# Two turned graph aggregations in three chunks of 512, 512 and 226 nodes for four, with the edge work one node tile later

## The chip, the cores and the metric

The kernel runs on one core of one Trainium2 chip. The metric is the device time of one execution in microseconds (us), taken over several runs. The engines are named as the profile names them: PE (matrix products; PEld are its weight loads), DVE (vector work), ACT (activations and copies), POOL (here almost wholly the issue of DMAs) and SP (nothing but DMA issues). A DMA is a transfer by the 16 DMA engines that all queues share.

## The reference

There are 1250 nodes with 1024 features and 20000 edges (src, dst), sorted by dst. All products are 1024 by 1024.

```
deg_inv = 1 / max(in-degree by dst, 1)
mean(h) = segment_sum(h[src], dst) * deg_inv
h   = relu(x @ W_self0 + mean(x) @ W_neigh0 + b0)
y   = layernorm(x + h @ W_self1 + mean(h) @ W_neigh1 + b1)
z   = y @ W.T + b                       # third layer: edges turned (src gathers dst), self loops added
out = layernorm(y + segment_sum(norm * z[dst], src)),   norm = dsqrt[src] * dsqrt[dst]
```

## The kernel before

**Adjacency as dense panels.** Sums over edges are done as matrix products with a 1250 by 1250 matrix of edge counts, padded to 10 node tiles of 128 and stored in DRAM as five panels of two tiles (256 columns, 1.28 MB each). There are two of them, adj_in (for the first two layers) and adj_out (for the third). POOL clears each with four large DMAs (L634) and then fills it by 160 indirect DMAs (the function put, L641), one for each column of 125 edges, all on one queue, first the 160 of adj_in and then those of adj_out. The 160 fall in 10 groups of 16; since the edges are sorted by dst, group g holds the edges whose dst is about 125g to 125g+125. A group may be put when DVE has finished repeats(g), which finds edges that occur more than once; its last instruction raises batch_ready (L980). Puts of adj_in raise one of the semaphores scattered_in, split by NEEDS: the numbers of groups after which the first, second, ... chunk of node columns is complete.

**Stages on PE.** (1) N0: x @ W_neigh0, ten node tiles one after the other (function linear, L1409). Each tile of x is first turned by PE (turn_tile), copied as a high part by ACT (turn_hi, L682) and a low part by DVE (turn_lo, L900). Results are split by evict_hi and evict_lo. In between, DVE does the edge work in the order its loop gives: edge_keys (waits for the edge list's DMA), edge_cells, edge_form, repeats. A one-column product (the small sum, L1402) on PE adds up the bad flags that edge_keys makes, for edge_form. (2) S0: x @ W_self0, turned, in three chunks CHUNKS0 of 4, 4 and 2 tiles (L1437); its blocks go to DRAM (s0t_scr). (3) The first turned aggregation, mean0 (L1468): for each chunk of CHUNKS, degrees by a product with ones (L1457), then for each of the eight feature blocks d twenty matmuls against the chunk's panels; the results stand in six PSUM banks in rotation, so block m waits for h_free m-5. DVE multiplies a block by 1/degree (L1169, which raises h_free), then adds the stored S0 block that SP has fetched (L1172, which waits for s0_in and raises h_sum), and so on in order; ACT applies the relu. (4) Two big products by a seven-product scheme (L1525). (5) MEAN1 (L1542). (6) The second turned aggregation, gather (L1559), against adj_out, chunk by chunk, each followed by a sum of scale factors (L1581) that waits for ten steps of DVE (L1281). (7) GCN: the last product, ten node tiles (L1409 again), with layer normalization and stores.

**SP's queue is in order.** The lines below are the part of SP's program that feeds stage 3. load_chunk_1(c) loads the panels of chunk c, after waits on the scatters of all groups that the chunk needs; what follows in the program, the fetches of S0 blocks (L512) among them, waits behind it.

```python
            sp.wait_ge(m1_full[0], 16)
            load_chunk_1(1)
...
            for m, (c, d) in enumerate(H_BLOCKS):
...
                sp.dma_start(fetch_slot(m)[:, 0:CHUNKS[c][1] * T], s0t_scr[d, :, lines(CHUNKS[c])]).then_inc(s0_in[m % 8], 16)
                if m in (15, 23):
                    load_chunk_1(2 + m // 17)
```

In the kernel before, chunks 0, 1, 2 and 3 of mean0 hold 256, 512, 256 and 226 nodes and need 3, 7, 9 and 10 groups.

Of the kernel before, what the change touches and what calls it, by code (L numbers as in the profile page):

```python
# [23 lines left out]
def build(nc, x, src, dst, w_self0, w_neigh0, b0, w_self1, w_neigh1, b1, w_gcn, b_gcn, out):  # L24
# [29 lines left out]
    MEAN1_PAIRS = (1, 2, 0, 1, 2, 0, 1, 2, 0, 2)  # L54
# [9 lines left out]
    PRODUCT_BANKS = ((0, 1, 2, 3, 4), (0, 1, 2, 3, 4), (5, 6, 7, 0, 1), (2, 3, 4, 5, 6), (7, 0, 1, 2, 3), (7, 0, 1, 2, 3), (4, 5, 6, 7, 0))  # L64
    assert NT == 2 * HALF and KD == 2 * KH and HALF == 5 and XOP + WOP <= OPS and HD == BANK

    with ExitStack() as ctx:
# [127 lines left out]
        def product_bank(g, i, p):  # L195
            return (PRODUCT_BANKS[i][p] + g) % 8

# [32 lines left out]
        def acc_pair(q, t):  # L230
            if q == N0:
                return t % 2
            if q == GCN:
                return (1, 3, 0)[t % 3]
            return MEAN1_PAIRS[t]

# [26 lines left out]
        scattered_in = sems("scattered_in", 4)  # L263
# [6 lines left out]
        m1_full = sems("m1_full", 4)  # L270
        p1_full = sems("p1_full", 3)
        m2_full = sems("m2_full", 4)
# [79 lines left out]
        for l in (N0, S0, GCN):  # L352
            for k in range(KD):
                raw_slot[l, k] = 4 + k % 2 if l == GCN else 2 + k if l == N0 and k >= 4 else k % 4
                loads[raw_slot[l, k]] += 1
                raw_count[l, k] = loads[raw_slot[l, k]]
# [4 lines left out]
        H_BLOCKS = [(c, d) for c in range(4) for d in range(KD)]  # L361
# [13 lines left out]
        def fetch_free(m):  # L375

            return m - 3 if m < 2 * KD else 2 * KD - 3 + m % 8 // 2 if m < 3 * KD else m - 7
# [31 lines left out]
        def _(sp):  # L409
# [9 lines left out]
            def load_panels(table, c, where, full):  # L419
                t0, n = CHUNKS[c]  # L420
# [5 lines left out]
            def load_tile(t):  # L426
                sp.dma_start(g_tile[:, t % 2, :, :].bitcast(F32), xt_scr[t, :, :, :]).then_inc(xt_full[t % 2], 16)
# [21 lines left out]
            def load_chunk_1(c):  # L449
                if c == 0:  # L450
                    sp.wait_ge(*last_use(6))
                elif c == 1:
                    sp.wait_ge(s0_full, 3 * KD)
                else:
                    sp.wait_ge(h_full, KD * (c - 1))
                    sp.wait_ge(dsum_done, sum(n for _, n in CHUNKS[:c - 1]) // 2)
# [18 lines left out]
            for i, (c, k) in enumerate(S0_STEPS):  # L475
# [24 lines left out]
                if i == 21:  # L500
                    load_chunk_1(0)
            sp.wait_ge(m1_full[0], 16)
# [4 lines left out]
            for m, (c, d) in enumerate(H_BLOCKS):  # L507
                for i in [S0_BLOCKS.index((b, d)) for b in {0: (0,), 1: (0, 1), 2: (1,), 3: (2,)}[c]]:
                    sp.wait_ge(s0_stored[i % 4], 16 * (i // 4 + 1))
                if m >= 4:  # L510
                    sp.wait_ge(h_sum, fetch_free(m))
                sp.dma_start(fetch_slot(m)[:, 0:CHUNKS[c][1] * T], s0t_scr[d, :, lines(CHUNKS[c])]).then_inc(s0_in[m % 8], 16)  # L512
                if m in (15, 23):
                    load_chunk_1(2 + m // 17)
# [10 lines left out]
            sp.wait_ge(h_sum, KD * 4)  # L525
# [36 lines left out]
            load_panels(adj_out, 0, m2_panels[0], m2_full)  # L562
# [17 lines left out]
            for t in range(NT):  # L580
                if t == 0:
                    sp.wait_ge(g_full, KD * 3)
                    sp.wait_ge(s_step, NT * 3)
                    for j in range(4):
                        sp.wait_ge(g_stored[j], 16 * 2)
                if t >= 2:
                    sp.wait_ge(acc_full, acc_index(GCN, t - 2) + 1)
                if t in [t0 for t0, n in CHUNKS[1:]]:
                    c = [t0 for t0, n in CHUNKS].index(t)
# [3 lines left out]
                if t == 1:  # L593
                    sp.wait_ge(w_lo_done, KD * GCN + 6)
                    load_w(GCN, 7)
                    for j in range(4):
                        sp.wait_ge(g_stored[j], 16 * KD)
                    sp.wait_ge(g_full, KD)
                    sp.wait_ge(s_step, NT)
                    for s in range(2):  # L600
                        sp.wait_ge(stored[s], 16 * NT // 2)
                        sp.dma_start(xin[:, s, :], y_scr[node_rows(s), :]).then_inc(res_full[s], 16)
                if t >= 2:
                    sp.wait_ge(acc_free, acc_index(GCN, t - 2) + 1)
                    sp.dma_start(xin[0:rows(t), t % 2, :], y_scr[node_rows(t), :]).then_inc(res_full[t % 2], 16)
# [71 lines left out]
        def _(act):  # L677
# [964 lines left out]
```

## Time and profile before

| what | value |
|---|---|
| median of 3 runs | 859.11 us (858.87 to 862.55) |
| the profiled execution, own time | 865.72 us |
| span of its trace, first to last instruction | 863.9 us |
| mean granted PE clock | 0.988 |
| PE busy | 838.9 us |
| POOL busy | 460.4 us |

The profile is of one execution, whose own time is 6.6 us above the median and 1.8 us above its span. A matmul's end is modelled, so differences of starts are the better measure of a rate. A clock of 1.0 is 2.4 GHz, 0.5 is 1.2 GHz; a number between is a mean over the stretch. "Idle before" names what ended an engine's wait, inferred from semaphores; "issue" means nothing that the profile shows.

### The profile page before, as it was taken

To read this page: it belongs to the slowest core of one execution; us is meant where nothing else is said; L and a number is where in the kernel's file an instruction comes from. 1 tells how busy PE (TensorE), PEld (TensorE's weight loads), DVE (VectorE), ACT (ScalarE), POOL (GpSimd) and SP (SyncE) were. 2 spreads that over 40 slices of the span, in tenths; PEclk is the share of its full clock that TensorE was granted. 3 is DMA by queue.
4 is the path that set the end of the run, shared out by engine and by line. 5 is a ranking of instruction groups with operands and counts; after the bars stand their busy time and mean duration, and the time that the engine had idled before them with its cause. 6 is when DMAs were issued, how large, how long until landed. Compare 5 with 4: busy or idle time off the path is not lost.

```text
span 863.9 us, 10999 instructions
## 1 busy us (share of the span) xinstructions
PE 838.9 (97%) x4295; PEld 714.8 (83%) x4295; DVE 461.6 (53%) x714; ACT 177.8 (21%) x218; POOL 460.4 (53%) x343
## 2 busy tenths in 40 slices
PE   8799999999999999999999999999999999999996
PEld 6588888888899889888888888778889789988885
DVE  5486567100015655698654478766655535455554
ACT  5011113020211111652303201312222213200000
POOL 4038886877878868886788788878720000000000
PEclk9899999999999999999999999999999999999999
DMA  9968938363578354388688477448778748655551
GB/s 297 384 244 313 315 112 263 95 197 80 150 214 265 80 134 109 93 322 288 240 278 316 155 284 255 102 127 219 213 248 276 224 147 274 226 195 195 195 189 44
DMA packets 99482, 180.56 MB, mean 209 GB/s; under 512 B 15474, under 2 KB 75898, under 8 KB 94048
## 3 DMA queue, kind: packets, MB, share of 16 engines
q1 hardware_dynamic: 60144, 124.17, 43.3%
q10 hardware_dynamic: 26896, 40.65, 13.3%
q0 software_dynamic: 12384, 14.95, 7.6%
q8 instruction: 38, 0.62, 0.3%
q14 instruction: 20, 0.16, 0.1%
HBM read 107.08 MB, written 72.43 MB: 208 GB/s over the span
## 4 chain that ended last, share of the span: by engine, by line
PE 86%; DMA 5%; DVE 4%; ACT 2%; issue 2%; ACTq 1%; POOL 0%; DVEq 0%; SPq 0%; POOLq 0%
PE ps L1409 22%; PE ps L1525 19%; PE ps L1437 12%; PE ps L1559 10%; PE ps L1468 10%; PE ps L1542 9%; DMA u<-edges_scr 3%; PE ps L1393 1%; DMA spare<-in_x 1%; ACT outb L743 1%; PE ps L1358 1%; PE ps L1348 1%; DMA edges_scr<-u 1%; PE ps L1457 1%; ACTq L733 0%
## 5 line engine op out<-in xcount | busy, mean ns | idle before, releaser
L641 POOL DMA_INDIRECT adj_out<-loops,idx_out x160 | 244.3, 1527 | 70.8 <-issue 64.6
L641 POOL DMA_INDIRECT adj_in<-mult,idx_in x160 | 200.4, 1252 | 89.3 <-issue 89.3
L1525 PE MATMUL ps<-u 128*128 128x512 f32 x840 | 190.7, 389 | 1.4 <-DVE u L1064 1.4
L1525 PEld LDWEIGHTS ps<-u 128*128 128x128 f32 x840 | 157.6, 188 | 34.2 <-issue 1.6
L1409 PE MATMUL ps<-wx 128*128 128x512 f32 x480 | 115.7, 399 | 1.7 <-ACT wx L700 1.2
L1437 PE MATMUL ps<-wx 128*128 128x512 f32 (+1 forms) x576 | 111.0, 355 | 1.6 <-ACT outb L743 1.6
L1437 PEld LDWEIGHTS ps<-wx 128*128 128x128 f32 x576 | 95.5, 193 | 17.1 <-ACT outb L743 2.1
L1409 PEld LDWEIGHTS ps<-wx 128*128 128x128 f32 x480 | 90.8, 192 | 22.3 <-ACT wx L700 2.3
L1409 PE MATMUL ps<-u 128*128 128x512 f32 x432 | 98.2, 389 | 0.0
L1542 PE MATMUL ps<-u,panel_tiles 128*128 128x512 f32 (+1 forms) x400 | 95.5, 398 | 1.9 <-DVE s L1131 1.9
L1468 PE MATMUL ps<-wx,u 128*128 128x256 f32 (+5 forms) x640 | 96.1, 312 | 0.0
L1409 PEld LDWEIGHTS ps<-u 128*128 128x128 f32 x432 | 81.0, 188 | 16.8
L1468 PEld LDWEIGHTS ps<-wx,u 128*128 128x128 f32 (+1 forms) x640 | 88.1, 194 | 6.6
L1542 PEld LDWEIGHTS ps<-u,panel_tiles 128*128 128x128 f32 (+1 forms) x400 | 75.6, 191 | 18.5 <-issue 2.3
L1559 PE MATMUL ps<-u,wx 128*128 128x512 f32 (+2 forms) x480 | 74.5, 317 | 0.0
L1559 PEld LDWEIGHTS ps<-u,wx 128*128 128x128 f32 x480 | 67.2, 191 | 6.6
L1161 DVE TENSOR_SCALAR dinv_row<-ps 128x256 f32<-128x256 f32 (+2 forms) x4 | 1.9, 479 | 99.3 <-PE ps L1457 99.3
L826 ACT ACTIVATE std<-mv,eps 128x1 f32<-128x1 f32 x20 | 5.9, 295 | 165.5 <-DVE mv L1007 165.5
L743 ACT ACTIVATE outb<-ps,b0c 128x512 f32<-128x512 f32 (+1 forms) x24 | 14.8, 618 | 102.2 <-PE ps L1437 90.3
L1325 DVE SCALAR_TENSOR_TENSOR outb<-ps,dscale,xin 128x1024 f32<-128x1024 f32 x9 | 11.6, 1284 | 40.6 <-PE ps L1409 40.6
L798 ACT ACTIVATE ht<-ht 128x256 f32<-128x256 f32 (+2 forms) x32 | 14.9, 465 | 80.3 <-DVE ht L1172 80.3
L1169 DVE TENSOR_TENSOR ht<-ps,dinv_row 128x256 f32<-128x256 f32 (+2 forms) x32 | 15.3, 479 | 25.3 <-PE ps L1468 25.1
(168 smaller groups left out, 737.7 us busy)
## 6 DMA issues: line engine op xcount, KB each, us to landing
left_scr<-u SPq DMA_DIRECT2D x7, 2560.0 KB, 9.7
u<-left_scr SPq DMA_DIRECT2D x7, 2560.0 KB, 9.6
xt_scr<-wx ACTq DMA_DIRECT2D x10, 1024.0 KB, 9.9
u<-xt_scr SPq DMA_DIRECT2D x10, 1024.0 KB, 4.9
wx<-xt_scr SPq DMA_DIRECT2D x16, 512.0 KB, 3.6
adj_in<-u POOLq DMA_DIRECT2D x4, 1600.0 KB, 22.9
adj_out<-u POOLq DMA_DIRECT2D x4, 1600.0 KB, 14.1
wx<-adj_in SPq DMA_DIRECT2D x5, 1280.0 KB, 6.8
```

The costliest lines, as they stand in the source:

```text
L641: pool.indirect_dma_start(table, bass.IndirectOffsetOnAxis(ap=index[0:EP, j:j + 1], axis=0), counts[0:EP, j:j + 1], None, bounds_check=CEL ...
L743: nc.scalar.activation(staged[i % 4][:, 0:width], ps[:, d, 0:width], ACT.Identity, bias=b0c[:, d:d + 1]).then_inc(s0_free, 1)
L798: nc.scalar.activation(cell, cell, ACT.Relu).then_inc(h_done, 1)
L1169: nc.vector.tensor_tensor(cell, ps[:, h_bank(m), 0:width], row, ALU.mult).then_inc(h_free, 1)
L1325: nc.vector.scalar_tensor_tensor(z, pair_bank(acc_pair(GCN, t))[:, :], dscale[:, t:t + 1], rest, ALU.mult, ALU.add).then_inc(acc_free, 1)
L1348: ins = nc.tensor.transpose(ps[:, 4 + k // 4, k % 4 * T:(k % 4 + 1) * T], xin[:, t % 2, k * P:(k + 1) * P], ident[:, :])
L1409: ins = nc.tensor.matmul(acc[:, cols], left_tile[:, t % 2, k, left * T:(left + 1) * T], w_row(q, k, right)[:, cols], start=(i == 0), stop= ...
L1437: ins = nc.tensor.matmul(block_of[d], w[:, k, left, d * P:(d + 1) * P], where[right], start=(first and left + right == 0), stop=(final and ...
L1468: ins = nc.tensor.matmul(ps[:, h_bank(m), 0:width].rearrange("p (n j) -> p n j", n=n // 2), typed(u0_part(k, h, d), exact), typed(panels[0 ...
L1525: ins = nc.tensor.matmul(ps[:, product_bank(g, i, p), :], left_op[n % 2][:, p, k, left, :], right_op[n % 2][:, k, right, :], start=(not on ...
L1542: ins = nc.tensor.matmul(pair_bank(acc_pair("MEAN1", t))[:, cols], typed(p1_tile[t][0:rows(k), k, :], exact), typed(u[0:rows(k), n, k, h, ...
L1559: ins = nc.tensor.matmul(ps[:, g_bank(KD * c + d), 0:width].rearrange("p (n j) -> p n j", n=n // 2), typed(yd[:, h, d * P:(d + 1) * P], ex ...
```

## The change

Both turned aggregations go over three chunks instead of four. mean0 uses CHUNKS0: 512, 512 and 226 nodes, which need 5, 9 and 10 groups of edges. gather takes the small chunk (226 nodes) first, then 512 and 512. Panels of two chunks of mean0 and of the gather move to other addresses; the weight rows of the last product that these addresses overlap are split later (rows 3 and 4 after the gather's second chunk, rows 5 to 7 after its end). The last product takes its node tiles in the order of LAST_TILES. In stage 1, edge_keys moves from the end of node tile 0 to tile 1 (behind turn_lo(2)), edge_cells and edge_form from tile 1 to tile 2, repeats(0) from tile 1 to tile 3, and the small sum on PE from tile 1 to tile 2. PSUM banks are renamed to suit (MEAN1_PAIRS, BANK_ORDER), and the counts in waits are adapted. The diff, cut to its core:

```diff
-    CHUNKS = ((0, 2), (2, 4), (6, 2), (8, 2))
     CHUNKS0 = ((0, 4), (4, 4), (8, 2))
-    NEEDS = (3, 7, 9, GROUPS)
+    CHUNKS = ((8, 2), (0, 4), (4, 4))
+    NEEDS = (5, 9, GROUPS)
+    LAST_TILES = (0, 1, 8, 9, 2, 3, 4, 5, 6, 7)
...
-    MEAN1_PAIRS = (1, 2, 0, 1, 2, 0, 1, 2, 0, 2)
+    MEAN1_PAIRS = (0, 1, 2, 0, 1, 2, 0, 1, 0, 2)
+    BANK_ORDER = (4, 5, 0, 1, 2, 3, 6, 7)
...
-        m1_panels = [panels_at(wx, OPS + PSIZE * i, n) for i, n in ((0, 1), (1, 2), (0, 1), (2, 1))]
+        m1_panels = [panels_at(wx, OPS + PSIZE * i, n) for i, n in ((0, 2), (2, 2), (0, 1))]
-        m2_panels = [panels_at(panel_tiles, PER, 1), panels_at(u_flat, XT_AT - 2 * PSIZE, 2), panels_at(u_flat, XT_AT, 1),
-                     panels_at(u_flat, XT_AT - PSIZE, 1)]
+        m2_panels = [panels_at(panel_tiles, PER, 1), panels_at(u_flat, XT_AT - 4 * PSIZE, 2), panels_at(u_flat, XT_AT - 2 * PSIZE, 2)]
...
-            return (PRODUCT_BANKS[i][p] + g) % 8
+            return BANK_ORDER[(PRODUCT_BANKS[i][p] + g) % 8]
...
-        H_BLOCKS = [(c, d) for c in range(4) for d in range(KD)]
+        H_BLOCKS = [(c, d) for c in range(3) for d in range(KD)]
...
             def load_chunk_1(c):
                 if c == 0:
-                    sp.wait_ge(*last_use(6))
+                    sp.wait_ge(*last_use(7))
...
                 for b in range(c + 1):
                     sp.wait_ge(scattered_in[b], 16 * RUN * (NEEDS[b] - (NEEDS[b - 1] if b else 0)))
-                load_panels(adj_in, c, m1_panels[c], m1_full)
+                load_panels(adj_in, CHUNKS0[c], c, m1_panels[c], m1_full)
...
-                if i == 21:
+                if i == 23:
                     load_chunk_1(0)
-            sp.wait_ge(m1_full[0], 16)
+            sp.wait_ge(m1_full[0], 32)
             load_chunk_1(1)
...
-                if m in (15, 23):
-                    load_chunk_1(2 + m // 17)
+                if m == 15:
+                    load_chunk_1(2)
...
-            for c in range(1, 4):
-                if c == 3:
-                    sp.wait_ge(g_full, KD * 2)
-                    sp.wait_ge(s_step, NT * 2)
-                load_panels(adj_out, c, m2_panels[c], m2_full)
-                for k in {1: (2, 3), 2: (4, 5), 3: (6,)}[c]:
-                    sp.wait_ge(w_lo_done, KD * GCN + k - 1)
-                    load_w(GCN, k)
+            for c in range(1, 3):
+                load_panels(adj_out, CHUNKS[c], c, m2_panels[c], m2_full)
+            for k in (2, 3, 4):
+                sp.wait_ge(w_lo_done, KD * GCN + k - 1)
+                load_w(GCN, k)
...
+                elif l == GCN and k < 3:
+                    act.wait_ge(acc_full, acc_index("MEAN1", NT - 1) + 1)
                 elif l == GCN and k < 5:
-                    act.wait_ge(acc_full, acc_index("MEAN1", NT - 1) + 1)
-                elif l == GCN and k == 5:
                     act.wait_ge(g_full, 2 * KD)
                     act.wait_ge(s_step, 2 * NT)
                 elif l == GCN:
-                    act.wait_ge(g_full, 32)
-                    act.wait_ge(s_step, 4 * NT)
+                    act.wait_ge(g_full, 3 * KD)
+                    act.wait_ge(s_step, 3 * NT)
...
                     turn_lo(t + 1)
                     if t == 1:
+                        edge_keys()
+                    elif t == 2:
                         edge_cells()
                         edge_form()
-                        repeats(0)
-                    elif t >= 2:
-                        repeats(t - 1)
+                    elif t >= 3:
+                        repeats(t - 3)
                     evict_lo(N0, t)
-                    if t == 0:
-                        edge_keys()
...
-            for g in range(NT - 2, GROUPS):
+            for g in range(NT - 4, GROUPS):
                 repeats(g)
...
-                    if q == N0 and t == 1 and i == 20:
+                    if q == N0 and t == 2 and i == 16:
                         pe.wait_ge(bad_ready, 1)
```

## Rows read from the trace of the kernel before

**Rows 1.** The page: busy time of the engines, first line

```profile
PE 838.9 (97%) x4295; PEld 714.8 (83%) x4295; DVE 461.6 (53%) x714; ACT 177.8 (21%) x218; POOL 460.4 (53%) x343
```

**Rows 2.** Timeline of PE, 0 to 70 us: start, us, instructions [idle before]

```profile
39.53 0.19 PE L1402 MATMUL ps<-ones_nt,bad 125*1 125x1 f32 x2 [6.11 <-DVE bad L920]
39.65 6.48 PE L1409 MATMUL ps<-wx 128*128 128x512 f32 x16
...
46.75 11.17 PE L1409 MATMUL ps<-wx 128*128 128x512 f32 x48
...
58.56 11.15 PE L1409 MATMUL ps<-wx 128*128 128x512 f32 x48
```

**Rows 3.** Windows: PE, PEld, DVE, ACT, POOL busy us; PE clock; DMA share, GB/s

```profile
39.50:46.10 6.60, 6.57 (x20) 5.17 (x21) 5.14 (x15) 1.02 (x1) 0.00 (x0) 0.57 1.01 431
```

**Rows 4.** Timeline of DVE, 8 to 100 us

```profile
36.30 1.32 DVE L910 SCALAR_TENSOR_TENSOR key<-u 125x1120 f32<-125x1120 int32 x1 [10.90 <-DMA u<-edges_scr]
...
47.27 0.96 DVE L968 TENSOR_TENSOR same_eq<-key 125x768 f32<-125x768 f32 x1
...
52.02 0.17 DVE L980 TENSOR_TENSOR idx_in<-idx_in,repeat 125x16 int32<-125x16 int32 x1
...
71.67 1.23 DVE L900 TENSOR_TENSOR wx<-ps,wx 128x1024 fp32r<-128x1024 f32 x1 [1.40 <-ACT wx L682]
```

**Rows 5.** The four clears of adj_in on POOL (line L634), issued 21.0 to 22.7 us

```profile
L634 POOL DMA_DIRECT2D adj_in<-u x4: 532/548/598, 21.0 to 22.7; - x4
...
DMA to landing us min/median/max: 18.1/22.9/32.7
```

**Rows 6.** Timeline of POOL, 0 to 200 us: the first scatter, and a pause

```profile
56.39 1.28 POOL L641 DMA_INDIRECT adj_in<-mult,idx_in  x1 [33.19 <-issue]
...
140.55 1.70 POOL L641 DMA_INDIRECT adj_in<-mult,idx_in  x1 [5.86 <-issue]
```

**Rows 7.** Windows of line L641 alone: scatters counted; then that line, 287 us on

```profile
56.30:289.30 233.00, 179.33 (x144) 0.99 0.63 194
...
L641 POOL DMA_INDIRECT adj_in<-mult,idx_in x2: 1192/1194/1196, 286.5 to 288.0; - x2
```

**Rows 8.** Line L641 over the whole span: issue to landing

```profile
DMA to landing us min/median/max: 2.5/3.5/21.0
```

**Rows 9.** Timeline of SP's DMA queue, 205 to 360 us

```profile
250.23 1.09 SPq L423 DMA_DIRECT2D wx<-adj_in  x2
251.42 5.32 SPq L512 DMA_DIRECT2D xin<-s0t_scr  x1
```

**Rows 10.** Timeline of DVE, 250 to 345 us

```profile
257.64 0.36 DVE L1169 TENSOR_TENSOR ht<-ps,dinv_row 128x256 f32<-128x256 f32 x1
264.55 0.42 DVE L1172 TENSOR_TENSOR ht<-ht,xin 128x256 f32<-128x256 f32 x1 [6.55 <-DMA xin<-s0t_scr]
```

**Rows 11.** Timeline of PE, 246 to 360 us: each chunk's degrees (L1457), then the products

```profile
251.96 1.43 PE L1457 MATMUL ps<-wx,ones_r 128*128 128x256 f32 x10 [1.80 <-ACT outb L743]
...
274.62 2.46 PE L1457 MATMUL ps<-wx,ones_r 128*128 128x512 f32 x10
...
314.80 1.35 PE L1457 MATMUL ps<-wx,ones_r 128*128 128x256 f32 x10
...
335.91 1.28 PE L1457 MATMUL ps<-wx,ones_r 128*128 128x226 f32 x10
...
357.20 2.97 PE L1525 MATMUL ps<-u 128*128 128x512 f32 x12 [1.43 <-DVE u L1064]
```

**Rows 12.** Timeline of PE, 645 to 752 us: the gather

```profile
671.56 0.61 PE L1581 MATMUL ps<-ones_nt,sacc 128*128 128x1 f32 x4 [0.72 <-DVE sacc L1281]
672.02 36.99 PE L1559 MATMUL ps<-u,wx 128*128 128x512 f32 x160
...
709.66 19.43 PE L1559 MATMUL ps<-u,wx 128*128 128x256 f32 x160
...
729.29 18.11 PE L1559 MATMUL ps<-u,wx 128*128 128x226 f32 x160
```

More of the change, by code:

```diff
@@ L353, in build @@
             for k in range(KD):
-                raw_slot[l, k] = 4 + k % 2 if l == GCN else 2 + k if l == N0 and k >= 4 else k % 4
+                raw_slot[l, k] = 1 if l == GCN and k == KD - 1 else 4 + k % 2 if l == GCN else 2 + k if l == N0 and k >= 4 else k % 4
                 loads[raw_slot[l, k]] += 1
@@ L417, in load_w, with load_panels @@
                 sp.dma_start(raw_slots[slot], weights[l][k * P:(k + 1) * P, :]).then_inc(raw_full[slot], 16)
-            def load_panels(table, c, where, full):
-                t0, n = CHUNKS[c]
+            def load_panels(table, chunk, c, where, full):
+                t0, n = chunk
                 for i in range(n // 2):
@@ L593, in _ @@
                 if t == 1:
[L594 to L602, printed above, removed]
+                    for k in (5, 6):
+                        sp.wait_ge(w_lo_done, KD * GCN + k - 1)
+                        load_w(GCN, k)
                 if t >= 2:
                     sp.wait_ge(acc_free, acc_index(GCN, t - 2) + 1)
-                    sp.dma_start(xin[0:rows(t), t % 2, :], y_scr[node_rows(t), :]).then_inc(res_full[t % 2], 16)
+                    sp.dma_start(xin[0:rows(tile), t % 2, :], y_scr[node_rows(tile), :]).then_inc(res_full[t % 2], 16)
             sp.wait_ge(stored[0], 16 * NT)
@@ L771, in right_high @@
                 if n < 2:
-                    act.wait_ge(h_full, KD * 3 + KH if n == 0 else KD * 4)
+                    act.wait_ge(h_full, KD * 2 + KH if n == 0 else KD * 3)
                 else:
@@ L865, in _ @@
                     store_g(m - 1)
-                if m in (4, 8, 12, 16, 20, 24):
-                    split_hi(GCN, m // 4 - 1)
-            store_g(31)
-            split_hi(GCN, 6)
-            split_hi(GCN, 7)
+                if m in (7, 9, 11, 18, 20):
+                    split_hi(GCN, (7, 9, 11, 18, 20).index(m))
+            store_g(23)
+            for k in range(5, KD):
+                split_hi(GCN, k)
             for t in range(NT):
@@ L875, in _ @@
                 s = t % 2
+                tile = LAST_TILES[t]
                 if t < NT - 1:
                     act.wait_ge(norm_done, NT + t + 1)
-                    act.dma_start(out[node_rows(t), :], outb[0:rows(t), s, :]).then_inc(stored[s], 16)
+                    act.dma_start(out[node_rows(tile), :], outb[0:rows(tile), s, :]).then_inc(stored[s], 16)
                 else:
@@ L882, in _ @@
                         act.wait_ge(norm_done, NT + t + 1 + n)
-                        act.dma_start(out[node_rows(t), cols], outb[0:rows(t), s, cols]).then_inc(stored[s], 16)
+                        act.dma_start(out[node_rows(tile), cols], outb[0:rows(tile), s, cols]).then_inc(stored[s], 16)
         @block.vector
@@ L915, in edge_keys @@
                 then_next(nc.vector.tensor_tensor(mult[0:EP, :], mult[0:EP, :], loops[0:EP, :], ALU.add))
-                for (t0, n), g in list(zip(CHUNKS, NEEDS))[:-1]:
+                for (t0, n), g in list(zip(CHUNKS0, NEEDS))[:-1]:
                     then_next(nc.vector.scalar_tensor_tensor(mult[0:1, 0:1], e_dst[0:1, g, WINDOW:WINDOW + 1], float((t0 + n) * T),
@@ L1185, in _ @@
                     right_sums(0, 0)
-                elif m == 27:
+                elif m == 19:
                     left_low(0)
@@ L1302, in _ @@
                     scale_done(c)
-                if m in (4, 8, 12, 16, 20, 24):
-                    split_lo(GCN, m // 4 - 1)
-            split_lo(GCN, 6)
-            split_lo(GCN, 7)
+                if m in (7, 9, 11, 18, 20):
+                    split_lo(GCN, (7, 9, 11, 18, 20).index(m))
+            for k in range(5, KD):
+                split_lo(GCN, k)
             for t in range(NT):
@@ L1366, in pair_free @@
                 elif q == "MEAN1":
-                    pe.wait_ge(acc_free, acc_index(q, 7 if t == NT - 1 else t - 3) + 1)
+                    pe.wait_ge(acc_free, acc_index(q, max(i for i in range(t) if MEAN1_PAIRS[i] == MEAN1_PAIRS[t])) + 1)
                 elif q == GCN and t < 3:
-                    pe.wait_ge(g_free, 28 + 2 * t)
+                    pe.wait_ge(g_free, 20 + 2 * t)
                 elif q == N0:
@@ L1447, in mean0 @@
             def mean0(exact):
-                for c, (t0, n) in enumerate(CHUNKS):
+                for c, (t0, n) in enumerate(CHUNKS0):
                     width = node_cols((t0, n))
@@ L1480, in product_bank_free @@
                 if i == 0 and g == 0:
-                    pe.wait_ge(h_free, 27 + p)
+                    pe.wait_ge(h_free, 19 + p)
                 elif i == 0 and p < 3:
@@ L1488, in product_bank_free @@
                 elif i == 2 and p < 3 and g == 0:
-                    pe.wait_ge(h_free, 32)
-                    pe.wait_ge(dcol_read, 4)
+                    pe.wait_ge(h_free, 24)
+                    pe.wait_ge(dcol_read, 3)
                 elif i == 2 and p < 3:
```

69 lines of the change are left out of this document (36 added, 33 removed).

## The prediction, made before the changed kernel ran

> **What bounds the kernel now.** I read the page first: PE is busy 97% of the span [rows 1], so a gain must be a PE wait that goes or PE work that shrinks, and a loss must be a new PE wait. Next the list of waits and PE's timeline: the one wait of any size is the small sum, which waits 6.11 us for the bad flags [rows 2]. DVE makes them, and DVE sits 10.90 us until the edge list lands at 36.30 [rows 4]. Then POOL, because the change asks for more groups of scatters earlier: POOL is no bottleneck by its busy time, but its 160 scatters of adj_in are a serial chain from 56.39 to past 300 us [rows 6, 7], and mean0 (252 to 357 us) lives off it. Last SP, DVE and PE around mean0 [rows 9 to 11], and PE in the gather [rows 12].
>
> **The change part by part.**
>
> *The small sum one tile later.* Its wait goes: the flags need the edge list (36.30) and 3.2 us of DVE, so 39.5; without the wait PE finishes tile 1 at 33.4 + 8 matmuls, about 35.2 (a tile's 48 matmuls and eight turns take 58.56 - 46.75 = 11.81 us [rows 2]; 0.23 us a matmul), and reaches step 16 of tile 2 near 43.5, when the flags lie ready. The wait also cost its aftermath: the 16 matmuls behind it took 6.48 us where 16 take 3.7 at 0.23 each, at a mean granted clock of 0.57, a mix of the two levels after 6 us of idle PE [rows 2, 3]. So PE gains 6.1 + 2.8 = 8.9 us by the end of N0, and mean0 can start at about 243 instead of 251.96 [rows 11]. Bounds: 6.1 if the clock falls anyway, 8.9 if not; I take 8.9, as nothing else stops PE there.
>
> *The edge work later.* repeats(0) now stands two tiles later in DVE's program, but DVE is no longer held by the edge list ahead of turn_lo(2). Tile 3 now starts at 35.2 + 11.8 = 47.0, and PE turns tile 4 at 48.8. DVE's turn_lo came 2.1 us after such a turn (the turn behind the last of the 48 matmuls from 58.56, at 69.6, and turn_lo at 71.67 [rows 2, 4]), so 50.9 to 52.1; repeats takes 52.19 - 47.27 = 4.9 us [rows 4], so group 0 is ready at 57.1, against 52.2. POOL's first scatter had waited for the last clear: 22.7 + 32.7 = 55.4, then 1.0 us to the put at 56.39 [rows 5, 6]. Now it starts at 58.1, some 2 us later. Bounds: 0 (the clear still ends last) and +6 (DMA is full until about 47 us [rows 3], and the store that turn_hi(4) waits for can be late). Nothing behind changes: one group of 16 takes 24 us of POOL and 5 of DVE.
>
> *Five and nine groups.* In the kernel before, 144 scatters (nine groups) had been issued by 288.0 [rows 7]; with 2 us and the median 3.5 to landing [rows 8] they land at T = 293.5. Chunk 1 of mean0 now needs these nine groups; before it needed seven. mean0 now starts at 243, and its first chunk takes what a 512 chunk takes, 314.80 - 274.62 = 40.2 us [rows 11], so PE wants chunk 1 at 283. That is 10 us before its edges are in DRAM. This wait sits in SP, and SP is in order: behind load_chunk_1(1) stand the fetches of S0 blocks, so chunk 0's additions on DVE wait too. In the kernel before, the same sequence took 264.55 - 250.23 = 14.3 us from the issue of the two panels to the first addition [rows 9, 10], the fetch landing behind the panels. So DVE adds block 0 at T + 14.3 = 307.8, multiplies block 1 at 309.2 (0.7 us each), and only that frees PE's block 7 (h_free 2). PE comes to block 7 at 243 + 40.2 less one block of 4.6, so 278.6, and idles some 30 us. It comes back at the low clock: block 7 costs 16 matmuls at 6.48 and 4 at 0.9, 7.4 us, so 316.6. The panels have landed by then, and DVE, which has two panel sums (about 3 us each) and a second fetch to work off, frees block 8's bank before PE has done the degrees. Chunk 1: 40.2, to 356.8. Chunk 2 up to the first product: 357.20 - 335.91 = 21.3 [rows 11], its last link being the same DVE work, to 378.1. Before: 357.20. **Loss up to the products: 20.9 us.** The 8.9 us gained in N0, and the merged chunks of mean0 (22.7 + 21.1 for two of 256, 40.2 for one of 512: 3.6 us), are used up in waiting for T.
>
> *The gather.* Two chunks of 256 cost 160 matmuls at 120 ns (709.66 plus 19.3), one of 512 costs 160 at 230 (672.02 plus 36.9), one of 226 at 112 [rows 12]. Merging saves 2 x 19.3 - 36.9 = 1.7. But the chunk that goes first is followed by a wait for DVE's ten steps (PE waits 0.72 for them [rows 12]), which start when the first six blocks are done, 120 matmuls in: a first chunk of 226 instead of 256 columns brings that forward by 120 x 8 ns = 1.0, and the 0.3 of the other 40 matmuls is lost in the wait. I take 1.7 - 0.4 = **1.3 us gained**; bounds 0.4 (the first chunk gains nothing) and 1.7. The Trainium skill, page "TensorE: Matmul & The Clock Gate", section "Back-to-back issue gap", gives N/2.4 + 2.5 ns: 109 ns for 256 columns and 216 for 512, so that merging two would give 2.6 ns per pair, 0.4 us for 160; by it the sum below would be about 1 us longer. The rows (120, 230) differ from it and decide.
>
> *At nothing.* The weight rows 5 to 7 are split after the gather's end, each by a copy on ACT and a subtraction on DVE of turn_lo's size (1.23 [rows 4]): about 3 us for the last block's own copies, then 1.2 a row, so the third is done some 6.6 us after the end. PE takes 4 matmuls for each of rows 0 and 1 and 6 for each later one (0.23 us each), so it asks for rows 5, 6 and 7 at about 6.7, 8.1 and 9.4 us: cover 2.5 us, beyond that PE waits one for one. The scatters of adj_out run some 2 us later, the PE work that hides them some 20 us later, so their cover grows. The four panels of the gather's two larger chunks are issued together at MEAN1's end and hide behind the first chunk (19 us) and the second (37 us); two panels and what follows took 14.3 us above. Order of tiles, bank names: same instructions.
>
> **Sum.** 20.9 - 1.3 = +19.6 us. On the profiled execution: span 863.9 to 883.5, own time 865.7 to 885.3. The runs lie 6.6 us below that execution; with the same difference to the median, 859.1 + 19.6 = **878.7 us**.
>
> **The rivals.**
>
> *Scatters in time (faster).* One mechanism: the ninth group lands so early that SP never holds PE. Then everything counts: 8.9 + 3.6 + 1.3 = 13.8, so 845. For it: POOL pauses (5.86 us at one put [rows 6]) and slow puts may not come again. Against: PE asks for h_free 2 at 278.6, so T + 15.7 must be below that, T = 263, 30 us earlier than worked out. Even 144 puts at the undisturbed 1.5 us (24 us a group) from 58.1, with the 2.5 us of the clears of adj_out in between, end at 277. It decides only from T = 274 down (there loss and gains cancel). 0.08.
>
> *Only the panels are late.* If the additions do not hold PE (fetches in before the wait, or h_free ahead of it), PE does all of chunk 0 and waits just for the panels, T + 12 = 305.5: 305.5 + 40.2 + 21.3 = 367.0, +9.8 - 1.3 = +8.5, so 867.6. Against it: DVE's order, and the 14.3 us [rows 9, 10]. 0.12.
>
> *Later still.* Group 0 at +6, panels and fetches slower together, or the weight rows uncovered: +4 to +8, so 883 to 887. 0.08.
>
> *The wait is there but small (same).* T near 276 by faster puts: 859 within 4. 0.04.
>
> **How the numbers follow.** The forecast has 0.68: 878.7, with T from -8 (the pauses gone) to +4, so 870 to 883. The range for 8 in 10 takes in most of the two neighbours: 864 to 885. About 0.5% (4.3 us) is what a measurement tells here. Faster 0.08, same 0.04, slower 0.68 + 0.12 + 0.08 = 0.88.
>
> **What would show it.** Right: PE's wait on bad is gone and the clock in 33 to 46 us is whole; a PE wait of 25 to 32 us at a L1468 block in mean0, ended by DVE's L1169, with a low clock behind it; SP's issue of two adj_in panels near 293; the first put near 58; products from about 378; the gather some 1 us shorter. Wrong: puts at another pace, nine groups landed well before 290, or SP issuing the S0 fetches ahead of the panels; then the time moves one for one with T.

## The result, and the profile after

The changed kernel takes **878.23 us** (median of 4 runs, 877.63 to 879.50) against 860.77 beside it (858.87 to 862.55): ratio **1.0197**, 95% interval 1.0168 to 1.0227, so some 17 us slower. The forecast was 878.7. The profiled execution took 877.63, with a span of 875.9.

The page's chain of work that ended last, its two lines (by engine, by line):

```profile
PE 58%; POOL 18%; issue 10%; DMA 9%; DVE 3%; ACT 1%; SPq 1%; POOLq 0%; ACTq 0%; DVEq 0%
PE ps L1521 19%; POOL adj_in L636 17%; PE ps L1405 11%; PE ps L1555 10%; PE ps L1538 9%; PE ps L1464 6%; DMA adj_in<-u 4%; DMA first_rows<-in_L_gnn_W_neigh 2%; DMA spare<-in_x 1%; PE ps L1389 1%; DMA xin<-s0t_scr 1%; PE ps L1354 1%; DMA xt_scr<-outb 1%; POOLq L636 0%; DVE spare L1132 0%
```

The scatters of adj_in (L636, L641 before) are now 17% of the chain: from the first put to the 144th it holds only them and the gaps between them (part of its "issue"). Ahead of them stands the clear of adj_in ("DMA adj_in<-u", 4%). PE's waits (engine, line and what it waited for: us in total, times, longest):

```profile
PE ps L1464 <- DVE ht L1164: 22.9, 1, 22.9
PE ps L1577 <- DVE sacc L1276: 3.4, 1, 3.4
PE ps L1453 <- DMA wx<-adj_in: 2.8, 1, 2.8
```

The wait for bad [rows 2] is not among them. PE's timeline, N0 and then mean0 (compare [rows 2, 11]):

```profile
42.69 0.19 PE L1398 MATMUL ps<-ones_nt,bad 125*1 125x1 f32 x2
...
241.61 2.55 PE L1453 MATMUL ps<-wx,ones_r 128*128 128x512 f32 x10 [2.78 <-DMA wx<-adj_in]
...
258.83 18.63 PE L1464 MATMUL ps<-wx,u 128*128 128x512 f32 x80
300.35 6.90 PE L1464 MATMUL ps<-wx,u 128*128 128x512 f32 x20 [22.90 <-DVE ht L1164]
307.09 2.46 PE L1453 MATMUL ps<-wx,ones_r 128*128 128x512 f32 x10
...
347.33 1.28 PE L1453 MATMUL ps<-wx,ones_r 128*128 128x226 f32 x10
```

The small sum runs at 42.69 without a wait, and the granted clock around it (33 to 46 us) is 1.00. mean0 starts at 241.61, does 140 of its first chunk's 160 matmuls, and stops 22.9 us for h_free at block 7. The 20 matmuls behind the stop take 6.90 us at a clock of 0.67. Windows, 33 to 46 us and behind the stop (columns as in [rows 3]):

```profile
33.00:46.00 13.00, 13.00 (x63) 10.52 (x63) 9.19 (x25) 2.06 (x2) 0.00 (x0) 1.00 1.00 418
...
300.30:307.00 6.70, 6.65 (x20) 5.30 (x21) 2.60 (x2) 0.69 (x2) 5.22 (x5) 0.67 1.07 350
```

What releases that stop, read backwards through three timelines: DVE, SP, POOL (compare [rows 6, 7, 9, 10]):

```profile
299.00 0.69 DVE L1167 TENSOR_TENSOR ht<-ht,xin 128x512 f32<-128x512 f32 x1 [49.27 <-DMA xin<-s0t_scr]
299.61 0.68 DVE L1164 TENSOR_TENSOR ht<-ps,dinv_row 128x512 f32<-128x512 f32 x1
...
287.23 1.08 SPq L425 DMA_DIRECT2D wx<-adj_in  x2
288.41 2.82 SPq L514 DMA_DIRECT2D xin<-s0t_scr  x1
...
58.83 1.27 POOL L636 DMA_INDIRECT adj_in<-mult,idx_in  x1 [36.28 <-issue]
...
248.68 1.19 POOL L636 DMA_INDIRECT adj_in<-mult,idx_in  x1 [2.48 <-issue]
...
58.70:286.00 227.30, 175.29 (x144) 0.99 0.54 164
```

DVE frees the bank by the multiplication at 299.61, behind its first addition, which sat 49.27 us until the first S0 block was there. That fetch left SP at 288.41, behind two adj_in panels that SP could only ask for at 287.23. The 144 scatters of nine groups, from 58.83, are all put by 286 (the last row counts the puts in a window).

The gather, PE's timeline and one line of ACT's (compare [rows 12]):

```profile
661.06 18.20 PE L1555 MATMUL ps<-panel_tiles,wx 128*128 128x226 f32 x160
682.65 0.61 PE L1577 MATMUL ps<-ones_nt,sacc 128*128 128x1 f32 x4 [3.39 <-DVE sacc L1276]
683.12 38.58 PE L1555 MATMUL ps<-u,wx 128*128 128x512 f32 x160
...
722.35 36.98 PE L1555 MATMUL ps<-u,wx 128*128 128x512 f32 x160
...
680.78 0.38 ACT L857 ACTIVATE outb<-ps 128x256 fp32r<-128x256 f32 x1 [4.29 <-DMA xt_scr<-outb]
```

It takes 98.9 us (661.06 to 759.98) against 96.2. The wait behind its first chunk grew from 0.72 to 3.39, and the first 512 chunk takes 1.6 us more than the second, at a granted clock of 0.83 in its first 10 us.

### The profile page after: what moved, and what is told of

The parts are those of the page before. It is cut to its first block, busy times and chain, and to the rows that moved or that the text cites. A ratio compares the mean times of both kernels' runs of the same rounds, so it can differ in the third digit from the quotient of the medians.

```text
span 875.9 us, 10210 instructions
## 1 busy us (share of the span) xinstructions
PE 830.5 (95%) x3965; PEld 692.8 (79%) x3965; DVE 455.5 (52%) x675; ACT 174.8 (20%) x202; POOL 450.5 (51%) x343
## 4 chain that ended last, share of the span: by engine, by line
PE 58%; POOL 18%; issue 10%; DMA 9%; DVE 3%; ACT 1%; SPq 1%; POOLq 0%; ACTq 0%; DVEq 0%
PE ps L1521 19%; POOL adj_in L636 17%; PE ps L1405 11%; PE ps L1555 10%; PE ps L1538 9%; PE ps L1464 6%; DMA adj_in<-u 4%; DMA first_rows<-in_L_gnn_W_neigh 2%; DMA spare<-in_x 1%; PE ps L1389 1%; DMA xin<-s0t_scr 1%; PE ps L1354 1%; DMA xt_scr<-outb 1%; POOLq L636 0%; DVE spare L1132 0%
## 5 line engine op out<-in xcount | busy, mean ns | idle before, releaser
L636 POOL DMA_INDIRECT adj_out<-loops,idx_out x160 | 240.4, 1502 | 75.2 <-issue 70.4
L636 POOL DMA_INDIRECT adj_in<-mult,idx_in x160 | 194.4, 1215 | 90.6 <-issue 90.6
L1464 PE MATMUL ps<-wx,u 128*128 128x512 f32 (+1 forms) x480 | 94.9, 358 | 22.9 <-DVE ht L1164 22.9
L1405 PE MATMUL ps<-wx 128*128 128x512 f32 x480 | 113.2, 393 | 2.6 <-ACT wx L695 2.0
L1464 PEld LDWEIGHTS ps<-wx,u 128*128 128x128 f32 x480 | 79.4, 192 | 37.0 <-DVE ht L1164 23.3
L1433 PEld LDWEIGHTS ps<-wx 128*128 128x128 f32 x576 | 93.9, 189 | 16.8 <-ACT outb L738 1.8
L1405 PEld LDWEIGHTS ps<-wx 128*128 128x128 f32 x480 | 88.9, 188 | 22.5 <-ACT wx L695 3.5
L1555 PE MATMUL ps<-u,wx 128*128 128x512 f32 (+1 forms) x320 | 75.6, 398 | 0.0
L1555 PEld LDWEIGHTS ps<-u,wx 128*128 128x128 f32 (+1 forms) x320 | 61.2, 192 | 13.6
L1167 DVE TENSOR_TENSOR ht<-ht,xin 128x512 f32<-128x512 f32 (+1 forms) x24 | 14.2, 594 | 54.1 <-DMA xin<-s0t_scr 53.4
L793 ACT ACTIVATE ht<-ht 128x512 f32<-128x512 f32 (+1 forms) x24 | 13.3, 553 | 107.6 <-DVE ht L1167 107.6
```

The lines of the kernel that those rows point to most:

```text
L636: pool.indirect_dma_start(table, bass.IndirectOffsetOnAxis(ap=index[0:EP, j:j + 1], axis=0), counts[0:EP, j:j + 1], None, bounds_check=CEL ...
L793: nc.scalar.activation(cell, cell, ACT.Relu).then_inc(h_done, 1)
L1167: nc.vector.tensor_tensor(cell, cell, fetch_slot(m)[:, 0:width], ALU.add).then_inc(h_sum, 1)
L1405: ins = nc.tensor.matmul(acc[:, cols], left_tile[:, t % 2, k, left * T:(left + 1) * T], w_row(q, k, right)[:, cols], start=(i == 0), stop= ...
L1433: ins = nc.tensor.matmul(block_of[d], w[:, k, left, d * P:(d + 1) * P], where[right], start=(first and left + right == 0), stop=(final and ...
L1464: ins = nc.tensor.matmul(ps[:, h_bank(m), 0:width].rearrange("p (n j) -> p n j", n=n // 2), typed(u0_part(k, h, d), exact), typed(panels[0 ...
```

## The experiments

**Theory A**: T, the time from which SP may ask for chunk 1's panels (nine groups landed), sets the start of the products one for one, through SP's order and DVE's first addition. PE time won before it is spent in waiting. **Rivals**: the parts of the change simply add up; or the stop has another cause (the panels, the fetches, the banks of a 512 chunk) and would be there with the scatters in time.

Times are medians; ratios are to the kernel before on the same chip, with 95% intervals.

| run | us | ratio | what it is |
|---|---|---|---|
| e1_edges_only | 855.04 | 0.9935 (0.991 to 0.9961) | edge work and small sum later, alone |
| e10_edges_again | 854.25 | 0.9924 (0.9901 to 0.9946) | the same |
| e2_mean0_only | 879.33 | 1.0216 (1.0189 to 1.0242) | three-chunk mean0 alone |
| e3_gather_only | 865.16 | 1.0036 (1.0009 to 1.0062) | three-chunk gather alone |
| e9_old_gather | 877.72 | 1.0203 (1.0174 to 1.0233) | changed kernel, gather as before |
| e5_edges_early | 882.72 | 1.0226 (1.0184 to 1.0268) | changed kernel, edge work as before |
| e4_fetch_first | 877.52 | 1.0190 (1.0164 to 1.0217) | changed kernel, S0 fetches ahead of the panels |
| e6_puts_later | 893.50 | 1.0367 (1.0322 to 1.0412) | changed kernel, groups 5 to 9 put later |
| e7_two_groups_out | 857.59 | 0.9946 (0.9923 to 0.9969) | changed kernel, two groups of edges left out |
| e8_edges_gather_split | 854.18 | 0.9903 (0.9871 to 0.9936) | e1 with a gather in three chunks, panels in two steps |
| e11_edges_split_again | 857.60 | 0.9946 (0.9922 to 0.9971) | the same |
| e12_before_again | 863.40 | - | kernel before, second profile |

**The parts alone.** e1 takes this part of the change, e2 and e3 the others:

```diff
                     if t == 1:
+                        edge_keys()
+                    elif t == 2:
                         edge_cells()
                         edge_form()
-                        repeats(0)
-                    elif t >= 2:
-                        repeats(t - 1)
+                    elif t >= 3:
+                        repeats(t - 3)
```

> The kernel before with the edge work and the small sum one node tile later, and nothing else of the change. Theory A (the loss of the whole change is the wait for nine groups of scatters, and what PE gains ahead of it is used up there): alone the move is worth its full gain, since chunk 1 of mean0 still needs seven groups: PE's wait for the bad flags and the low clock behind it go, some 9 us, so about 852. Rival B (the later edge work makes the scatters late, and that is the loss): no gain or a loss, 860 or more, with new PE waits in mean0.

> The kernel before with the three chunks in the first aggregation alone. Theory A: the whole loss is here. PE comes to its block 7 some 9 us later than in the changed kernel, but goes on at the same time, since nine groups land when they land: a PE wait of about 14 to 18 us at a block of mean0, products near 366 to 369, 874 to 878 in all. Rival B (late edge work): the scatters start at 56 as before, so hardly any loss, 857 to 862.

> The kernel before with the three chunks in the gather alone (small one first, order of the last tiles). The prediction's term was 1.3 us gained, 859.5. The trace of the changed kernel shows instead a 3.4 us wait behind the first chunk and a gather 2.7 us longer than before: 863.5. If the wait there came from the late start of the whole kernel's second half, it is not seen here and 859.5 stands.

mean0 alone carries the whole loss (+18.6 us by its ratio), the edge work alone gains 5.6 to 6.5, the gather alone loses 3.1 (its wait behind the first chunk is 3.47 in e3, as in the changed kernel). Added up the three make about +16, next to the whole's +17, so these times alone do not tell theory A from the rival that the parts add up. The products do: in e2 they start at 372.50, and 10.6 us (what e1 gains, below) earlier would be 361.9, but the changed kernel has them at 368.62. e1's PE timeline, mean0's start, its third chunk and the products; last, from e2's PE timeline, its products:

```profile
241.35 1.43 PE L1459 MATMUL ps<-wx,ones_r 128*128 128x256 f32 x10 [1.93 <-ACT outb L746]
...
304.22 1.35 PE L1459 MATMUL ps<-wx,ones_r 128*128 128x256 f32 x10
...
346.61 33.57 PE L1527 MATMUL ps<-u 128*128 128x512 f32 x147 [1.43 <-DVE u L1066]
...
372.50 22.72 PE L1529 MATMUL ps<-u 128*128 128x512 f32 x99 [1.47 <-DVE u L1068]
```

Products at 346.61 against 357.20 [rows 11]: without the three chunks the 10.6 us won in N0 reach the products whole. In the times only 5.6 to 6.5 of them show (855.04, where 852 was expected): the execution behind [rows 11] lay 4.1 us above the 861.62 beside e1, and e1's profiled one 1.7 below its own median. The chunk that needs nine groups starts at 304.22 and waits for nothing.

**The edge work back, inside the change** (the diff above, undone):

> The changed kernel with the edge work and the small sum back at their old places; both three-chunk aggregations stay. Theory A (the landing of the nine groups, T, sets the products' start, so PE time won in N0 is spent in waiting): PE stops again for the flags in N0, but the time stays within 3 us of the changed kernel's 878, 875 to 881; the wait in mean0 gets shorter by about what N0 loses. Theory B (the parts add up): the 5.7 us that the edge work gave alone are lost again, about 884.

The median lies nearest to B (884); by the ratios e5 is 2.5 us above the changed kernel, and its interval takes in both A's 881 and B's 884. The trace says A, with T itself moved. e5's stop in mean0, the issue of the panels, the products and a pause of POOL:

```profile
303.55 6.69 PE L1468 MATMUL ps<-wx,u 128*128 128x512 f32 x20 [13.77 <-DVE ht L1168]
...
290.72 1.08 SPq L428 DMA_DIRECT2D wx<-adj_in  x2
...
371.97 16.34 PE L1525 MATMUL ps<-u 128*128 128x512 f32 x71 [1.44 <-DVE u L1063]
...
252.10 1.20 POOL L639 DMA_INDIRECT adj_in<-mult,idx_in  x1 [6.02 <-issue]
```

mean0 starts 10.8 us later (252.38 against 241.61), and the stop shrinks from 22.90 to 13.77: 9.1 are absorbed. But T is 3.5 us later, although the first put is earlier (55.39 against 58.83), since POOL pauses 6.02 us where it paused 2.48, and loses 3.4 us more in the rest of the 144 puts (1.3 of it at an earlier pause, 5.24 for 3.98). In 244 to 254 us the DMA engines are 85% busy in e5 (mean0's first panels are loaded then, 10 us later than in the changed kernel) and 20% busy in the changed kernel. So of the edge work's gain inside the change, what is left comes by way of T.

**The old gather, inside the change:**

> The changed kernel with the gather in its old four chunks: the later edge work and the three-chunk mean0 alone. If the gather's three chunks cost 3 us, as they did alone and as the two traces show (98.9 against 96.2 us): 875, between 873 and 877. If the gather's loss is only a shift of what comes before it: 878 as the changed kernel.

877.72, ratio 1.0203: no difference from the changed kernel that the times can tell. In e9's trace the gather takes 96.2 us, and its wait is 0.73, so the 2.7 us stand in the traces. Alone (e3) they came out as 3.1 in the time. From the products to the end, the six traces with this gather (the changed kernel, e3 to e7) take 506.9 to 510.7 us and the six with the old one (the kernel before twice, e1, e2, e9, e10) 505.1 to 506.8: 3.3 us apart in the mean. In the time of the full change this cost is not settled.

**The dose: the puts 12 us later.**

```diff
             for g in range(GROUPS):
                 pool.wait_ge(batch_ready, g + 1)
+                if g == 4:
+                    pool.wait_ge(cleared_out, 16 * 4)
+                    for i in range(2):
...
+                        pool.dma_start(diagonal, ones_nt[:, 0:NT // 2], allow_slow_non_contiguous=True).then_inc(diagonal_set, 16)
+                    pool.wait_ge(diagonal_set, 32)
+                    for j in range(4):
+                        put(adj_out, idx_out, loops, j, scattered_out)
```

> The changed kernel, with the two diagonal writes and the first four scatters of adj_out moved from behind the 160 scatters of adj_in to before its fifth group of sixteen; the same work, but the groups 5 to 9 of adj_in are put some 6 us (the diagonal and its landing) plus 6 us (four scatters) later. Theory A: the nine groups land about 12 us later, and the time moves with it one for one: 878 + 12 = 890, between 887 and 893; the wait in mean0 grows from 22.9 to about 35 us. Rival (the wait comes from the panels and the fetches that share the DMA engines, or from the bank order, whenever the groups land): 878 to 881.

```profile
314.14 7.07 PE L1470 MATMUL ps<-wx,u 128*128 128x512 f32 x20 [33.23 <-DVE ht L1170]
...
301.33 1.08 SPq L428 DMA_DIRECT2D wx<-adj_in  x2
...
382.96 5.24 PE L1527 MATMUL ps<-u 128*128 128x512 f32 x22 [1.44 <-DVE u L1065]
...
262.73 1.19 POOL L639 DMA_INDIRECT adj_in<-mult,idx_in  x1 [2.41 <-issue]
```

In e6's timelines of PE, SP and POOL the panels are asked for 14.1 us later (the moved work costs 13.2 us at its place, where 12 were expected), the stop is 33.23, the products start 14.3 us later, and the median moves by 15.3 (893.5, half a microsecond above the range given). One for one, as far as the times tell: theory A.

**The wait taken away: two groups left out.**

```diff
-            for g in range(GROUPS):
+            for g in (0, 1, 2, 3, 4, 5, 6, 9):
...
-                    sp.wait_ge(scattered_in[b], 16 * RUN * (NEEDS[b] - (NEEDS[b - 1] if b else 0)))
+                    sp.wait_ge(scattered_in[b], 16 * RUN * (5, 2, 1)[b])
```

> The changed kernel without the scatters of groups 7 and 8 of adj_in (32 of 160): that part of the edges is left out of the first two layers' sums, and the second chunk's panels wait for the seven remaining groups of its nine. They land some 48 us earlier, near 245. Theory A: no PE wait in mean0, all that the change saves on PE shows: products start near 241.5 + 40.5 + 40.5 + 21 = 343.5 against 368.6, so 878 - 25 = 853, between 850 and 856. Rival (a first chunk of 512 columns also stops for the panels, the fetches or the banks): a wait of 8 us or more stays, 860 or above.

```profile
244.03 3.96 PE L1456 MATMUL ps<-wx,ones_r 128*128 128x512 f32 x10 [2.99 <-DMA wx<-adj_in]
...
285.88 2.48 PE L1456 MATMUL ps<-wx,ones_r 128*128 128x512 f32 x10
...
326.07 1.28 PE L1456 MATMUL ps<-wx,ones_r 128*128 128x226 f32 x10
...
347.37 32.92 PE L1524 MATMUL ps<-u 128*128 128x512 f32 x144 [1.43 <-DVE u L1062]
```

No stop inside mean0; the products start at 347.37 and the time falls by 20.6. The rival that a 512 chunk stops anyway is out. It missed 853 by 4.6: products 3.9 us later than expected, and a second half 1.9 us longer than the changed kernel's. And it shows something else. The four runs with the edge work later and four chunks (e1, e8, e10, e11) have their products at 344.92 to 347.54, no later than e7. From mean0's start to the products e7 takes 103.34 us, and they take 103.92 to 105.89 (e1 105.26), so merging saves 0.6 to 2.6. But e7 starts 2.7 later than e1, waiting 2.99 us for its two first panels, where e1 needs one, and its ten matmuls behind that wait take 3.96 us, where those of its second chunk take 2.48. (With the edge work later, mean0 starts at 241.6 to 244.0 in the runs with three chunks and at 241.0 to 242.3 in those with four.) **Even with all edges in time, three chunks gain next to nothing here.**

**The fetches ahead of the panels.**

```diff
             sp.wait_ge(m1_full[0], 32)
-            load_chunk_1(1)
+            sp.wait_ge(s0_full, 3 * KD)
...
                 sp.dma_start(fetch_slot(m)[:, 0:CHUNKS0[c][1] * T], s0t_scr[d, :, lines(CHUNKS0[c])]).then_inc(s0_in[m % 8], 16)
+                if m == 7:
+                    load_chunk_1(1)
```

> The changed kernel, with the panels of mean0's chunk 1 asked for behind the eight fetches of S0 blocks of chunk 0 instead of ahead of them. Theory A with the order of SP's queue as the second half of the wait: PE no longer stops at block 7 and waits only for the two panels, which landed at 298.3 where chunk 1 now starts at 307.1: about 9 us less, 869 to 870, the PE wait standing at the degrees of chunk 1 and ended by a DMA. Rival (the queue's order costs nothing, the nine groups alone do): 877 to 879.

```profile
302.75 4.11 PE L1455 MATMUL ps<-wx,ones_r 128*128 128x512 f32 x10 [16.86 <-DMA wx<-adj_in]
...
291.59 1.07 SPq L425 DMA_DIRECT2D wx<-adj_in  x2
...
365.92 22.27 PE L1523 MATMUL ps<-u 128*128 128x512 f32 x97 [1.43 <-DVE u L1061]
...
253.05 1.19 POOL L638 DMA_INDIRECT adj_in<-mult,idx_in  x1 [6.58 <-issue]
```

The mechanism does what it should: PE finishes chunk 0 and waits only for the panels, and from T to the products it is 74.3 us instead of 81.4. But T is 4.4 us later: the fetches now move at 244 to 255 us, while POOL puts, and POOL's pause there grows from 2.48 to 6.58. 2.7 us are left in the trace, 0.7 in the median. A miss by 8.

**The gather's panels in two steps.** On top of e1:

```diff
-            for c in range(1, 3):
-                load_panels(adj_out, CHUNKS[c], c, m2_panels[c], m2_full)
+            load_panels(adj_out, CHUNKS[1], 1, m2_panels[1], m2_full)
+            sp.wait_ge(g_full, KD)
+            sp.wait_ge(s_step, NT)
+            load_panels(adj_out, CHUNKS[2], 2, m2_panels[2], m2_full)
```

> The edge work later and the three-chunk gather, with mean0 in its old four chunks; and in the gather the two panels of the second 512 chunk are asked for only when the first chunk (226) and its ten steps are done, where the changed kernel asks for all four at once. If the gather's wait of 3.4 us and the low clock behind it come from the store of its first block, which shares the DMA engines with four panels of 1.28 MB: the wait falls to 1 us or less, the 512 chunk takes 37.0 instead of 38.6, the gather 95 us instead of 98.9, and the time is 853 to 855, at or below the 855.0 of the edge work alone. If it has another cause (the shorter first chunk leaves DVE too little time): the wait stays near 3.4 and the time is 857 to 859.

> The edge work and the small sum one tile later, nothing else, once more, beside the next run on the same chip: 855, between 853.5 and 856.5.

> The edge work later and the gather in three chunks with the last two panels asked for after the first chunk, once more. By the traces its gather takes 95.9 us against 96.3 with four chunks, so 0.4 us less than the run beside it, 854.6: no difference that the times can tell. If the merged chunks saved the 1.7 us that their matmuls save by themselves: 853.3.

e8's gather, a line of ACT and two of PE:

```profile
658.03 0.38 ACT L861 ACTIVATE outb<-ps 128x256 fp32r<-128x256 f32 x1 [2.36 <-DMA xt_scr<-outb]
...
659.91 0.61 PE L1581 MATMUL ps<-ones_nt,sacc 128*128 128x1 f32 x4 [1.46 <-DVE sacc L1280]
660.38 36.99 PE L1559 MATMUL ps<-u,wx 128*128 128x512 f32 x160
```

With two panels in flight instead of four, ACT waits 2.36 us for the block's store (4.29 in the changed kernel), PE waits 1.46 instead of 3.39, and the 512 chunk is back at 36.99. e11, the second run in two steps, has 1.05 and 36.98; the six traces with four panels at once have waits of 3.20 to 3.47 and 38.6 to 39.6. So the four panels at once cause the gather's loss; the wait of 1 us or less that was expected came nearly in e11, and not in e8. The gather is then 95.9 us (639.76 to 735.65), next to 96.2 with four chunks (97.1 in e11, whose first chunk stands behind a wait, below): again hardly anything gained by merging. In time e8 and e11 (0.9903, 0.9946) stand on both sides of e1 and e10. All four beat both kernels; they are not told apart.

e11's twelve runs fall in two heaps, 852.1 to 853.6 and 857.3 to 860.0, with one between. Its profiled run (858.7) shows a wait that e8's (853.3) does not have; timelines of POOL, SP and PE:

```profile
633.38 1.39 POOL L640 DMA_INDIRECT adj_out<-loops,idx_out  x1 [0.30 <-issue]
...
636.61 0.36 SPq L427 DMA_DIRECT2D panel_tiles<-adj_out  x1
...
643.97 20.23 PE L1559 MATMUL ps<-panel_tiles,wx 128*128 128x226 f32 x159 [4.59 <-DMA panel_tiles<-adj_out]
```

The last scatter of adj_out is put at 633.4, where e8 put it at 627.7, and the gather's first panel comes 4.6 us late. POOL's four pauses in that chain (last section) add up to 19.8 us in e11 and to 13.3 in e8. The PE time won in N0 has brought the second chain of 160 scatters to the edge of the path.

**The kernel before, profiled again.**

> The kernel before, unchanged, profiled a second time. Its runs lie between 857 and 866, and the execution shown ahead of the prediction took 865.7. If that spread comes from the wait for the flags (6.1 us there, 2.7 in one run with the same edge work) and from when the scatters of adj_out end, an execution near 860 has a span of some 858 with the flags' wait or the stretch from the products to the end shorter than in the first profile (6.1 us; 357.2 to 863.9, 506.7 us).

```profile
39.95 0.19 PE L1402 MATMUL ps<-ones_nt,bad 125*1 125x1 f32 x2 [7.03 <-DVE bad L920]
```

At 863.4, with a span of 861.7, it still isn't an execution near the median. Its wait is longer, not shorter, and the stretch from the products to the end is 505.5 us against 506.7. What makes the kernel before wander between 857 and 866 stays open. On record its times go with the mean granted clock: of the 19 runs beside e1, those up to 859 us have 0.995 to 0.997, those from 864 us on 0.986 to 0.988. 0.009 of 860 us are 8 us (an estimate), about the distance; where in the kernel the clock falls in the one and not in the other was not profiled.

## Why the prediction was right, and where its terms were off

| step | predicted | measured |
|---|---|---|
| mean0 starts | 243 | 241.61 |
| first put | 58.1 | 58.83 |
| T, nine groups landed | 293.5 | 287.2 |
| T to DVE's first addition | 14.3 | 11.8 |
| block 7 starts | 309.2 | 300.35 |
| block 7, at the low clock | 7.4 | 6.7 |
| chunk 1; chunk 2 to the products | 40.2; 21.3 | 40.2; 21.3 |
| products against before | +20.9 | +11.4 |
| gather against before | -1.3 | +2.7 |
| span against before | +19.6 | +12.0 |
| median against the median before | +19.6 | +17.5 |

**The mechanism held.** The stop came where it was put (block 7, ended by DVE behind the first S0 fetch behind the panels behind nine groups of scatters), with the low clock after it. The products follow T at 81.4 us in the changed kernel, 81.6 in e2, 81.3 in e5, 81.6 in e6 and 81.4 in e9, over a spread of 14 us in T. Of the rivals, "scatters in time" did not come, and e7, which makes it come, gives 857.6 and not 845, since the gains of 8.9, 3.6 and 1.3 behind that price came as 5.6 to 6.5, 0.6 to 2.6 and a loss; "only the panels are late" is what e4 builds: 63.2 us from PE's return (302.75) to the products, where 61.5 was taken. Of the prediction's own signs, PE's wait (22.9, for 25 to 32), SP's issue (287.2, for 293) and the products (368.6, for 378) came short, for the reasons that follow.

**Two terms of the stop were mis-sized.** T: the puts were taken at the pace of the kernel before, 231.6 us from the first to the 144th [rows 6, 7]. They took 225.8 (58.83 to 284.59), with fewer slow puts and shorter pauses. With a start 0.4 later than taken (58.83 for 56.39 + 2) and 2.6 us from the last of them to SP's issue in place of 3.5, that makes 6.3. The way from T to the first addition took 11.8, not 14.3. Together 8.8 of the 9.5 us by which the products were forecast late, the rest being block 7.

**The first put was hit by luck.** It was taken from repeats(0), 57.1 us and 1.0 more. But group 0 was ready at 56.6, and POOL went on waiting for the last clear of adj_in. DVE's timeline, and the four clears (line L629):

```profile
56.44 0.18 DVE L976 TENSOR_TENSOR idx_in<-idx_in,repeat 125x16 int32<-125x16 int32 x1
...
L629 POOL DMA_DIRECT2D adj_in<-u x4: 532/546/598, 20.3 to 22.0; - x4
...
DMA to landing us min/median/max: 18.6/26.6/35.8
```

The last clear was issued at 22.0 and landed 35.8 us later, at 57.8, 1.0 us ahead of the put; in the kernel before it took 32.7 us [rows 5]. In all fourteen traces the first put comes 0.9 to 1.1 us behind that landing, and the landing takes 34.9 to 36.4 us with the edge work later and 30.0 to 32.9 with it at its old place. The prediction had the clear only as its bound with no delay. Why the clear takes longer was not tried.

**The gather was wrong in sign.** "Hide behind the first chunk" was true of the panels' arrival and false of what they do to others on the way: the stores of the first four blocks share the DMA engines with four panels, ACT's next copies wait for the stores, and DVE's ten steps wait for ACT. The size of the merge itself was right: by starts, a chunk of 256 takes 19.26 us (709.66 to 728.92 in the kernel before) and one of 512 takes 36.82 (722.35 to 759.17), so two of 256 take 1.7 us more. The Trainium skill, page "TensorE: Matmul & The Clock Gate", section "Back-to-back issue gap", gives N/2.4 + 2.5 ns for a single isolated matmul, by which 160 merged pairs would save 0.4 us (an estimate). The trace, a stream of matmuls with weight loads, does not agree with it. The 1.0 us taken for the shorter first chunk did not come: from its start to the small sum, e8 takes 20.15 us with 226 columns and the kernel before 20.15 with 256.

**The number was hit by two errors that cancel.** The sum was 7.6 us too large against the trace (19.6 against 12.0). It was put on an execution of the kernel before that lay 6.6 us above the median, and carried to the median with that difference kept. The changed kernel's profiled execution lies at its own median, so the difference was not one that both kernels have. By their own times the two profiles are 877.63 - 865.72 = 11.9 apart, the medians 17.5.

**What the change does, in sum.** The edge work later is worth 6 us alone. The three-chunk mean0 wants the panels of nine groups at 282 us, and through SP's order the first S0 block just before 277.5, but SP can ask for them only at 287.2; it loses 25 us of PE time by the stop and the clock (22.9, and 6.7 for a block of 4.65), and would gain next to nothing without the stop. What the edge work won in N0 is mostly waited away: it is worth 1.6 us (e9 against e2) to 4.5 us (the changed kernel against e5), by the ratios 1.1 and 2.5, differences near what the times can tell. The three-chunk gather is even at best.

## What to carry to other kernels

When a stage lives off a serial producer, write down when each of its portions is due and when the consumer will ask for it; merging chunks moves the demand forward, and a gain ahead of that point only lengthens the wait. In an in-order queue, count what stands behind a wait: here the stop came 20 matmuls before the data that was late was needed at all. Make the sum against the median, or against several profiled executions, before trusting a difference of a few microseconds to one of them.

## What the runs showed of the hardware

POOL pauses at the same scatters of adj_in in every run that puts them all: the 49th, and then the 88th with mean0 in four chunks and the 120th in three, also where two other DMAs and four other scatters were put in before it (e6). In adj_out it pauses at the 40th, 79th, 118th and 157th, 39 apart, in every run that leaves their order alone (e6: the 44th, 83rd and 122nd). So the pauses go with the place in the chain and not with the time. How long they are goes with the DMA engines. The pause at the 49th, over all fourteen traces, is 2.4 to 2.5 us where they are 10 to 16% busy during it (e1, e6, e10), 3.7 to 4.1 at 40 to 47%, and 5.2 to 6.3 where they are full (the five runs with the edge work at its old place); the one at the 120th is 2.4 to 2.5 at 5 and 22% (e6, changed kernel) and 6.0 and 6.6 where they are full (e5, e4). What the pauses are was not tried.

An indirect scatter of 125 elements costs POOL 1.19 us and 0.30 us between two (medians in all fourteen traces, adj_out's up to 1.20), apart from slower ones of 1.3 to 3.8 us: 7 to 17 in a chain of adj_in, 45 to 51 in one of adj_out.
